# Attention probabilities transposed in half-height tiles, two key steps at a time

## The reference

```python
xq = (inputs_q @ wq + bq).reshape(B, S, H, D)          # H = 16, D = 128, S = 1024
xk = (inputs_q @ wk + bk).reshape(B, S, Hk, D)         # Hk = 4
xv = (inputs_q @ wv + bv).reshape(B, S, Hk, D)
qg = (xq * scale).reshape(B, S, Hk, G, D)              # G = 4
attn = jnp.einsum('bqhgd,bkhd->bhgqk', qg, xk)
attn = jax.nn.softmax(attn, axis=-1)
out = jnp.einsum('bhgqk,bkhd->bqhgd', attn, xv).reshape(B, S, H * D)
return out @ wo + bo
```

## Time and profile before

| | us |
|---|---|
| median of 3 runs | 1141.88 |
| lowest and highest | 1140.17, 1142.14 |
| the profiled execution | 1144.78 |
| its span, first to last instruction | 1142.9 |
| TensorE busy in the span | 1059.6 (93%) |
| VectorE busy | 751.3 (66%) |
| ScalarE busy | 599.2 (52%) |
| GpSimd busy | 564.3 (49%) |

### The profile page before, as it was taken

One profiled execution on the slowest core, in us unless ns is written; L12 is line 12 of the kernel. 1 busy time (PEld: TensorE's weight loads), 2 busy tenths in 40 slices (PEclk: granted clock), 3 DMA queues, 4 the chain that ended last, 5 costly groups with the idle time before them and its releaser, 6 DMA issues. The chain is left out here.

```text
span 1142.9 us, 16866 instructions
## 1 busy us (share of the span) xinstructions
PE 1059.6 (93%) x6276; PEld 893.9 (78%) x6276; DVE 751.3 (66%) x1312; ACT 599.2 (52%) x1027; POOL 564.3 (49%) x408
## 2 busy tenths in 40 slices
PE   5899999999999999999998899997977978999992
PEld 4788888888888888888886776654755778999992
DVE  4877665777457775667775644446778765777777
ACT  3566654666446665456662424333422255777772
POOL 1664623756136563355540347772314776644453
PEclk9999999999999999999999899999988998999997
DMA  8400210002501672000001146631200457666665
GB/s 198 49 29 1 54 40 1 19 10 46 48 1 40 209 216 52 1 1 1 1 1 39 43 146 217 212 125 55 106 2 5 157 190 239 205 226 222 224 208 203
DMA packets 45634, 109.84 MB, mean 96 GB/s; under 512 B 8519, under 2 KB 26069, under 8 KB 43504
## 3 DMA queue, kind: packets, MB, share of 16 engines
q1 hardware_dynamic: 38640, 95.46, 29.1%
q0 software_dynamic: 6912, 13.30, 3.1%
HBM read 94.27 MB, written 41.29 MB: 119 GB/s over the span
## 5 line engine op out<-in xcount | busy, mean ns | idle before, releaser
L422 POOL TENSOR_TENSOR at_prob<-at_prob,at_inv_sum 128x1024 f32<-128x1024 f32 x128 | 243.6, 1905 | 286.4 <-DVE at_inv_sum L647 286.4
L612 ACT ACTIVATE at_pt_h<-ps 128x512 fp32r<-128x512 f32 x256 | 139.1, 596 | 152.4 <-PE ps L537 152.3
L697 DVE TENSOR_TENSOR at_pt_l<-ps,at_pt_h 128x512 fp32r<-128x512 f32 x256 | 164.6, 685 | 64.5 <-ACT at_pt_h L612 64.5
L686 DVE TENSOR_REDUCE at_neg_max<-ps 128x1 f32<-128x1024 f32 x128 | 154.7, 1209 | 36.3 <-PE ps L41 35.9
L579 ACT ACTIVATE at_prob<-ps,at_neg_max 128x1024 f32<-128x1024 f32 x128 | 143.6, 1122 | 17.9 <-DVE at_neg_max L686 17.9
L537 PE MATMUL ps<-ident,at_prob 128*128 128x128 f32 x1024 | 133.8, 274 | 3.8 <-POOL at_prob L422 3.8
L2072 POOL DMA_INDIRECT lines<-f_y,f_x_raw x96 | 97.1, 1011 | 81.0 <-ACT f_y L1990 51.9
L537 PEld LDWEIGHTS ps<-ident,at_prob 128*128 128x128 f32 x1024 | 120.1, 141 | 21.1 <-POOL at_prob L422 4.7
L39 PE MATMUL ps<-at_k_h,at_q_h 128*128 128x512 f32 x256 | 109.0, 426 | 0.0
L39 PE MATMUL ps<-at_pt_h,at_v_h 128*128 128x512 f32 x256 | 101.1, 395 | 0.0
L41 PE MATMUL ps<-at_pt_h,at_v_l 128*128 128x512 f32 x256 | 100.8, 394 | 0.0
(11 more groups left out here) (308 smaller groups left out, 2546.7 us busy)
## 6 DMA issues: line engine op xcount, KB each, us to landing
e_raw<-in_we SPq DMA_DIRECT2D x32, 624.0 KB, 4.2
f_cw_row<-cw SPq DMA_DIRECT2D x32, 512.0 KB, 3.9
slots<-in_empty SPq DMA_DIRECT2D x4, 3456.0 KB, 43.9
f_x_raw<-slots SPq DMA_DIRECT2D x32, 432.0 KB, 4.8
lines<-in_empty SPq DMA_DIRECT2D x3, 2048.0 KB, 32.8
f_e_raw<-in_we SPq DMA_DIRECT2D x32, 128.0 KB, 2.2
at_wq_raw<-in_wq SPq DMA_DIRECT2D x4, 512.0 KB, 3.7
at_wo_raw<-in_wo SPq DMA_DIRECT2D x4, 512.0 KB, 3.5
```

The source lines that it names most:

```text
L422: nc.gpsimd.tensor_tensor(prob[:, t % RING, :], prob[:, t % RING, :], inv_sum[:, t:t + 1].broadcast_to([P, T]), ALU.mult).then_inc(normed, 1)
L612: nc.scalar.activation(pt_h[:, e[1] % PT, :], turned(e[1]), ACT.Copy).then_inc(pt_high, 1)
L686: nc.vector.tensor_reduce(neg_max[:, t:t + 1], slot(n, start), AX.XY, ALU.max, negate=True).then_inc(maxed, 1)
L697: nc.vector.tensor_tensor(pt_l[:, e[1] % PT, :], turned(e[1]), pt_h[:, e[1] % PT, :].bitcast(F32), ALU.subtract).then_inc(pt_split, 1)
```

## The change

A pair of transpose steps is now issued together. Each block of 128 queries x 128 keys becomes two transposes of 64 queries: the upper 64 rows of `prob` against a 64x64 piece of the identity into bank 4, the lower 64 into bank 5. After a pair, bank h holds the h-th half of the queries of all four blocks, first for the even key step, then for the odd one. TensorE waits once, ahead of the even step, for both evictions of the pair before, and signals once, behind the odd step, by 2. ScalarE and VectorE still move one bank per step, now a half of the queries for both key steps. `pt_h` and `pt_l` become a ring of two pairs, and a product step reads its moving operand as two pieces of 256 columns, so that the columns of `o_bank(u)` are ordered half, block, query. ScalarE and VectorE put them back in order where they write `o_h` and `o_l`.

```diff
-        pt_h, pt_l = sb("pt_h", [P, PT, BANK], F32R), sb("pt_l", [P, PT, BANK], F32R)
+        pt_h, pt_l = sb("pt_h", [P, PT // 2, 2, BANK], F32R), sb("pt_l", [P, PT // 2, 2, BANK], F32R)
...
-        def turned(j):
-            return ps[:, 4 + j % 2, :]
+        HROWS = P // 2
+        def turned(h):
+            return ps[:, 4 + h, :]
+        def stored(pt, step):
+            return pt[:, step // 2 % (PT // 2), step % 2, :]
+        def moving(pt, step):
+            return pt[:, step // 2 % (PT // 2), :, step % 2 * D:(step % 2 + 1) * D]
+        def queries(ap):
+            return ap.rearrange("p (i h q) -> p h i q", i=4, h=2)
+        def outputs(u):
+            return o_bank(u).rearrange("p (h i q) -> p h i q", i=4, h=2)
...
-                            pe.wait_ge(pt_split, LIFT + own * STEPS + e[1] - 1)
+                            if kt % 2 == 0:
+                                pe.wait_ge(pt_split, LIFT + own * STEPS + e[1])
                             for i in range(4):
-                                last = nc.tensor.transpose(turned(e[1])[:, i * P:(i + 1) * P],
-                                                           prob[:, (4 * u + i) % RING, kt * P:(kt + 1) * P], net.ident[:, :])
-                            last.then_inc(pt_full, 1)
+                                at = kt % 2 * D + i * HROWS
+                                for h in range(2):
+                                    half = slice(h * HROWS, (h + 1) * HROWS)
+                                    last = nc.tensor.transpose(turned(h)[:, at:at + HROWS],
+                                                               prob[half, (4 * u + i) % RING, kt * P:(kt + 1) * P],
+                                                               net.ident[half, half])
+                            if kt % 2:
+                                last.then_inc(pt_full, 2)
...
-                            pe.wait_ge(pt_split, LIFT + g * STEPS + e[1] + 1)
+                            pe.wait_ge(pt_split, LIFT + g * STEPS + e[1] // 2 * 2 + 2)
-                            product(nc, o_bank(u), v_h[:, keys], v_l[:, keys], pt_h[:, e[1] % PT, :], pt_l[:, e[1] % PT, :],
+                            product(nc, o_bank(u).rearrange("p (h c) -> p h c", h=2), v_h[:, keys], v_l[:, keys], moving(pt_h, e[1]), moving(pt_l, e[1]),
...
-                            act.wait_ge(pv_done, LIFT + own * STEPS + e[1] - PT + 1)
-                            nc.scalar.activation(pt_h[:, e[1] % PT, :], turned(e[1]), ACT.Copy).then_inc(pt_high, 1)
+                            act.wait_ge(pv_done, LIFT + own * STEPS + e[1] // 2 * 2 - PT + 2)
+                            nc.scalar.activation(stored(pt_h, e[1]), turned(e[1] % 2), ACT.Copy).then_inc(pt_high, 1)
...
-                            nc.scalar.activation(o_h[:, u // NB, (u % NB) * BANK:(u % NB + 1) * BANK], o_bank(u),
+                            nc.scalar.activation(queries(o_h[:, u // NB, (u % NB) * BANK:(u % NB + 1) * BANK]), outputs(u),
...
-                            nc.vector.tensor_tensor(pt_l[:, e[1] % PT, :], turned(e[1]), pt_h[:, e[1] % PT, :].bitcast(F32),
+                            nc.vector.tensor_tensor(stored(pt_l, e[1]), turned(e[1] % 2), stored(pt_h, e[1]).bitcast(F32),
...
-                            nc.vector.tensor_tensor(o_l[:, u // NB, cols], o_bank(u), o_h[:, u // NB, cols].bitcast(F32),
+                            nc.vector.tensor_tensor(queries(o_l[:, u // NB, cols]), outputs(u), queries(o_h[:, u // NB, cols]).bitcast(F32),
```

## The result

The changed kernel took 1147.02 us (median, 1143.69 to 1150.54), the kernel before beside it 1142.01 (1139.33 to 1142.96): a ratio of 1.0041, 95% interval 1.0024 to 1.0059. It is about 5 us slower, where 2 us faster was forecast. The profiled execution of it took 1150.54 us, with a span of 1148.7.

The account below looks back on a forecast made before the run. TensorE, busy 93% of the span, was taken to bound the kernel. Saving 4.9 us on 123 pairs, less 0.9 and 2.0 for waits, gave 1139.9, say 1140 us; the eight-in-ten range was 1133 to 1190.

Parts of the forecast that it names:

- the sum itself: Whole kernel: 123 pairs at 0.04 save 4.9 us, waits lose 0.9 and 2.0; 2.0 us gained.
- the rival of the pieces: Attention products: moving operand in two pieces of 256 costs 0.01 us each, 8 us for 768, giving 1148; chance 0.08.
- Half-height transposes: Attention's transposes: two halves run side by side, 0.061 us a block in place of 0.109, saving 0.38 a pair.
- The prediction's own sign of being wrong: Profile after: sixteen halves over 0.7 or under 0.6 us, no gap, or products behind the pair moving from 0.23.
- The slow-load rival: Each half's load takes 0.107 us or halves' loads stand in line; 1189 or about 1200 us; chance 0.16.
- Two changes of shape: Around each transpose pair: entering and leaving half-height shape opens load gaps, costing 0.34 us; new stretch 1.30 against 1.34.
- the rival without a change of shape: Transpose pairs: loads at 64 rows run ahead as now, 0.39 us saved a pair, 1096 us; chance 0.06.
- Pieces of the moving operand: Attention products: reading the moving operand as two pieces of 256 columns costs nothing.
- The seven pairs: Pairs following a q projection whose low part delays VectorE: waiting for both banks loses 0.13 x 7 = 0.9 us.
- The closing: Closing pairs, without score products between: turns of 2.72 us, three losing 0.4 each; 2.0 lost with the last product pair.

Follow-up runs that it names:

- the pieces: 2 MB fills of `lines` cut from three into eight of 768 KB: changed kernel 1141.27 us (ratio 0.9976), kernel before 1140.19 (0.9968).
- the run with increments behind the transposes: Kernel before with 16 more semaphore increments per transpose pair on TensorE, behind the transposes, 2048 in all: 1180.35 us, ratio 1.0301.
- the run with the waits alone: Kernel before, full transposes kept, with only the change's waits for both banks and one signal per pair: 1153.71 us, ratio 1.0082.

## Why the prediction was wrong

The step that failed is the sum itself: it has no term for TensorE's supply of instructions. The prediction counted 2048 halves by their time in the array, listed what costs nothing, and never asked what it takes to bring 2048 more instructions. In its place the runs showed a stall of 3.48 us whose turn is 6.1 us longer, where the kernel before has one of 1.53 us and 3.35: 2.9 us net in the two profiles. With the supply mended by the pieces, the ratio of the changed kernel falls from 1.0041 to 0.9976, and the two kernels are alike: 0.9976 and 0.9968. The forecast for the array and the waits alone was -2.0 us, and measured is -0.7 (-4.4, +1.4, +2.3).

That the rival of the pieces named 1148, next to the measured 1147, is chance: its mechanism didn't occur, as the third point below shows.

- *Half-height transposes: right.* 16 halves take 0.71 us, less the last record of 0.22 that is 0.49, against 0.06 + 7 x 0.061 = 0.49. The prediction's own sign of being wrong, over 0.7 us for sixteen halves, is met by a hundredth. Its 0.65 left out the 0.06 of the first load, which its sum has; so the sign was set too tight, and the sum stands. The slow-load rival is out: its turn would be 0.35 longer than before.
- *Two changes of shape: right.* The stretch is 1.29, forecast 1.30; the rival without a change of shape is out.
- *Pieces of the moving operand: right.* The rival that they cost does not hold: a product with `at_pt_l` still takes 0.23 us (208.49 to 208.72).
- *The seven pairs: right in place, too small for three.* Four turns lose 0.09, which is the forecast 0.13 less the 0.04 saved. Three, where an output is also evicted, lose 0.35; the sum is 1.4 in place of 0.6. This term was mis-sized because the prediction read only the first and the last of the seven; the last section shows what differs in the three.
- *The closing: right.* 2.73 a turn, forecast 2.72; 2.3 us with the last product pair, forecast 2.0.
- *The first pair* was not looked at. The prediction left out that TensorE comes to it from a wait and at half clock. How long that lasts differs: the first turn took 6.3 to 7.9 us in kernels that don't change it, so this term may be chance (the run with increments behind the transposes left out).

Open in part is what lies behind the attention. From the last product of the output weights to the end of the span the profiles of all fourteen kernels take 521.6 to 528.4 us, with no order between changed and unchanged ones, though the program there computes the same. This time goes with the clock. In the shortest, the changed kernel with the pieces, the granted clock is 0.50, the 1.2 GHz level, for 49 us of it; in the longest, the run with the waits alone, for 69; in the changed kernel for 66, and in the kernel before for 57. Why the clock is low for longer in one execution than in another, no run shows. One profile can't tell 3 us by its end; the turns inside the attention can.

## What to carry to other kernels

Count instructions as well as their time: where a change adds many short ones to a busy engine, work out how long a packet of program lasts, and look for transfers longer than that which run at the same time. A long fill that nobody waits for can be cut into pieces; here that is worth about 4 us without the change and 7 with it (the differences of the ratios). A trade of two halves for one whole in the array must pay for both changes of shape, 0.34 of the 0.38 us it saved here.

## What the runs showed of the hardware

- Across a 2 MB fill that ran for about 33 us, the packets of TensorE's program started 30 to 46 us apart (the last two fills of every kernel that has them), and nine stalls ended 2.2 to 2.8 us behind the start of the late packet.
- A stall of 1.5 to 3.5 us with the reason issue made its turn 3 to 7 us longer, because the clock went to half behind it.
- A subtraction of VectorE with both operands in the state buffer and one of GpSimd ran in turn, not together. First VectorE's and GpSimd's rows of the changed kernel, with TensorE's next transposes behind them; then the two engines' rows of the run with the waits alone and of the kernel before, each merged by time from the timelines of both engines:

```profile
80.03 1.27 POOL L426 TENSOR_TENSOR at_wkv_l<-at_wkv_raw,at_wkv_h 128x512 fp32r<-128x512 f32 x1
80.14 2.25 DVE L680 TENSOR_TENSOR at_q_l<-at_proj,at_q_h 128x1024 fp32r<-128x1024 f32 x1
82.31 0.68 DVE L729 TENSOR_TENSOR at_o_l<-ps,at_o_h 128x512 fp32r<-128x512 f32 x1
82.91 1.27 DVE L723 TENSOR_TENSOR at_pt_l<-ps,at_pt_h 128x512 fp32r<-128x512 f32 x2
...
84.24 0.71 PE L561 MATMUL ps<-ident,at_prob 64*128 64x64 f32 x16 [0.32 <-DVE at_pt_l L723]
```

```profile
79.31 1.22 DVE L656 TENSOR_TENSOR at_q_l<-at_proj,at_q_h 128x1024 fp32r<-128x1024 f32 x1
79.40 2.29 POOL L406 TENSOR_TENSOR at_wkv_l<-at_wkv_raw,at_wkv_h 128x512 fp32r<-128x512 f32 x1
```

```profile
78.77 1.28 POOL L406 TENSOR_TENSOR at_wkv_l<-at_wkv_raw,at_wkv_h 128x512 fp32r<-128x512 f32 x1
79.11 2.01 DVE L654 TENSOR_TENSOR at_q_l<-at_proj,at_q_h 128x1024 fp32r<-128x1024 f32 x1
```

Whichever starts second takes longer: behind by 0.11 us, VectorE takes 2.25 against 1.22; behind by 0.09, GpSimd takes 2.29 against 1.27; and in the kernel before VectorE, behind by 0.34, takes 2.01. The Trainium skill ("SBUF — State Buffer", section "SBUF: two separate sides") says that these two engines share a port pair, that the first to start holds it for the whole instruction and the other waits; the rows agree. This is what differs in the three of the seven pairs. In the kernel before VectorE came second there too, but a pair needed only the first bank. In the changed kernel the pair needs both, VectorE's second subtraction ends at 84.18, and the pair starts at 84.24; the turn takes 3.98 in place of 3.63. With the waits alone VectorE starts first, and these three turns take 3.61 to 3.63, no longer than before.
